# Last attention unit in four groups of four heads, and the mixing products over 128 rows

## What is computed

```python
h = einsum("bct,bcd->bdt", x, W[condition])           # a 32x32 mixing matrix per sequence
q = (h @ Wq_c.T + bq_c) @ Wq_up.T + bq_up             # 32 heads of 192
kv = h @ Wkv_c.T + bkv_c                              # 64 latent columns + 64 shared ones
scores = q . k / sqrt(192);  attn = softmax(scores)   # over the 32 tokens of a sequence
x = x + (attn @ v) @ Wo.T + bo                        # summed over the heads
x = x + ffn(convolution(x, taps), dequantised weights)
```

## Time and profile before

| | |
|---|---|
| median of 3 runs | 785.07 us |
| the profiled execution | 785.16 us |
| its span on the core | 783.4 us |
| PE busy (products) | 758.1 us, 97% |
| PE weight loads (PEld) | 599.0 us, 76% |
| DVE busy | 617.0 us, 79% |
| ACT busy | 377.4 us, 48% |
| GpSimd (POOL) busy | 199.1 us, 25% |

### The profile page before, as it was taken

The page is one execution under the profiler, slowest core; times in us unless marked ns, Lnnn a source line. Parts: engine busy times, 40 slices in busy tenths (PEclk is TensorE's granted clock), DMA queues, the critical chain, the costliest instruction groups (busy, mean ns, idle before and its releaser), DMA issues.

```text
span 783.4 us, 18621 instructions
## 1 busy us (share of the span) xinstructions
PE 758.1 (97%) x7821; PEld 599.0 (76%) x7821; DVE 617.0 (79%) x1109; ACT 377.4 (48%) x675; POOL 199.1 (25%) x203
## 2 busy tenths in 40 slices
PE   7999999999999999999999999999999699999996
PEld 5776777778677767868686777778676599999996
DVE  4476789988998786778777766968888578888887
ACT  2375546455563675565454636445674322222221
POOL 5002020011002000262200000000042388888871
PEclk9899999999999999999999999999999899999999
DMA  9910010010002000000400010002206159899861
GB/s 230 238 49 5 2 59 2 1 31 30 2 2 59 1 2 2 28 2 10 90 3 2 2 55 2 2 2 58 82 2 184 65 127 201 204 202 205 203 132 69
DMA packets 42739, 51.74 MB, mean 66 GB/s; under 512 B 7024, under 2 KB 29600, under 8 KB 42656
## 3 DMA queue, kind: packets, MB, share of 16 engines
q1 hardware_dynamic: 40384, 49.87, 25.9%
q0 software_dynamic: 1056, 0.49, 0.3%
q10 hardware_dynamic: 1216, 0.19, 0.1%
HBM read 41.91 MB, written 8.63 MB: 65 GB/s over the span
## 4 chain that ended last, share of the span: by engine, by line
PE 90%; DVE 5%; ACT 3%; issue 2%; another core or an unknown queue 1%; POOL 0%; DVEq 0%
PE ps L730 33%; PE ps L599 9%; PE ps L600 8%; PE ps L601 8%; PE ps L778 7%; PE ps L797 4%; PE ps L1063 4%; PE ps L1064 4%; PE ps L616 3%; PE ps L1032 2%; PE ps L693 1%; DVE z_low L1423 1%; PE ps L1020 1%; PE ps L1022 1%; PE ps L1021 1%
## 5 line engine op out<-in xcount | busy, mean ns | idle before, releaser
L1163 ACT ACTIVATE qt<-ps,m_bias 128x512 f32<-128x512 f32 x228 | 145.5, 684 | 96.4 <-PE ps L730 96.4
L730 PE MATMUL ps<-q_high,m_high 64*128 64x512 f32 x768 | 154.5, 398 | 2.4 <-ACT qt L1163 1.3
L730 PE MATMUL ps<-q_high,m_low 64*128 64x512 f32 x768 | 150.8, 388 | 0.0
L730 PE MATMUL ps<-q_low,m_high 64*128 64x512 f32 x768 | 108.3, 387 | 0.0
L1423 DVE TENSOR_TENSOR z_low<-ps,z_high 128x512 fp32r<-128x512 f32 x128 | 79.7, 682 | 15.9 <-ACT z_high L1182 15.9
L730 PEld LDWEIGHTS ps<-q_high,m_high 64*128 64x128 f32 x768 | 72.6, 184 | 24.5 <-issue 8.7
L730 PEld LDWEIGHTS ps<-q_low,m_high 64*128 64x128 f32 x768 | 72.7, 184 | 14.7
L529 POOL TENSOR_TENSOR o_sum<-o_part,o_part 128x512 f32<-128x512 f32 x7 | 9.1, 1303 | 294.0 <-ACT o_part L1192 294.0
L730 PEld LDWEIGHTS ps<-q_high,m_low 64*128 64x128 f32 x768 | 72.7, 185 | 13.6
L1182 ACT CAST z_high<-ps 128x512 fp32r<-128x512 f32 x128 | 66.8, 597 | 22.9 <-PE ps L797 22.9
L1168 ACT ACTIVATE sc<-sc 128x512 f32<-128x512 f32 x60 | 37.3, 631 | 46.6 <-DVE sc L1408 41.1
(11 more groups left out here) (292 smaller groups left out, 1646.0 us busy)
## 6 DMA issues: line engine op xcount, KB each, us to landing
x_in<-in_x SPq DMA_DIRECT2D x16, 512.0 KB, 3.6
x_s<-in_x SPq DMA_DIRECT2D x32, 256.0 KB, 5.7
out<-res SPq DMA_DIRECT2D x31, 256.0 KB, 3.6
toep_high<-taps_scratch SPq DMA_DIRECT2D x32, 192.0 KB, 4.3
toep_low<-taps_scratch SPq DMA_DIRECT2D x32, 192.0 KB, 5.0
toep_far<-taps_scratch SPq DMA_DIRECT2D x32, 64.0 KB, 5.5
wq_nope<-in_L_attn_Wq_up SPq DMA_DIRECT2D x2, 768.0 KB, 10.1
wq_nope<-in_L_attn_Wq_up SPq DMA_DIRECT2D x1, 1536.0 KB, 16.3
```

Of the source, the lines that this page charges most:

```text
L730: mm = pe.matmul(ps[:, fold_bank(u, j) + e, :], weights[rows, (GH * g + j) // 2, c, :], moving[c][rows, :], start=start, stop=stop)
L1163: act.activation(qt[:, j, :], ps[:, fold_bank(u, j) + j % 2, :], ACT.Identity, bias=m_bias[:, h:h + 1]).then_inc(s["qt_done"], 1)
```

## The change

It has two parts.

**Mixing.** `mixed_x(i)` makes 8 products of 128 rows and 128 columns. The two banks now hold two token quarters each, so the first bank is ready after half of the products; `mixed_high` and `mixed_low` copy 512 contiguous columns, and `project_ca` waits before its first and its third token quarter, for three and for four `h_low`.

**The last unit.** Its 16 heads go in four groups q of four. `scores_last(q)` makes 16 products of 128 columns into one bank, at least one pair of heads behind the fold of its group; `begun_last` and `ended_last` on DVE and `soft_last` on ACT treat one group; `values_last(h)` takes two groups and makes products of 64 columns. Units 14 and 15 use other PSUM banks, so some waits go or come.

```diff
+    LATE_ZBANK = ((BX, BZ, BZ + 1, BO), (BZ, BZ + 1, BT, BS))
-    LAST_SBANK = ((BS, BS + 1), (BZ, BZ + 1))
+    LAST_SBANK = (BX, BZ, BX, BT + 1)
...
-                for tt in range(TT):
-                    for g in range(2):
-                        for e in range(2):
-                            rows, o = slice(64 * e, 64 * e + 64), tt * P + 64 * g
-                            mm = pe.matmul(ps[:, MIX_BANK(i, e), o:o + 64], x_in[i % 2][rows, g, tt * P:(tt + 1) * P],
-                                           mix_of(i)[rows, g, rows], start=True, stop=True)
-                            if tt == TT - 1 and g == 1:
-                                mm.then_inc(s["h_ready"], 1)
+                for n in range(2):
+                    for t_ in range(2):
+                        for g in range(2):
+                            tt = 2 * n + t_
+                            o = t_ * HT + g * P
+                            mm = pe.matmul(ps[:, MIX_BANK(i, n), o:o + P], x_in[i % 2][:, g, tt * P:(tt + 1) * P],
+                                           mix_of(i)[:, g, :], start=True, stop=True)
+                    mm.then_inc(s["h_ready"], 1)
...
-                pe.wait_ge(s["h_low_done"], 4 * k + 4)
                 for tt in range(TT):
+                    if tt % 2 == 0:
+                        pe.wait_ge(s["h_low_done"], 4 * k + 3 + tt // 2)
                     mm = three(ps[:, BZ + 1, :], wcT_high[:, tt, 1, :], wcT_low[:, tt, 1, :], h_high[:, :, tt, :],
                                h_low[:, :, tt, :], tt == 0, tt == TT - 1)
...
-                    if u == LAST and j == GH // 2:
-                        pe.wait_ge(s["s_taken"], 4 * LAST + 4)
-                    if u == LAST and j == GH // 2 + 2:
-                        pe.wait_ge(s["zl_done"], 8 * (LAST - 1) + 6)
...
-            def scores_half(h, n):
-                pe.wait_ge(s["qt_done"], qt_count(LAST, 8 * h + 8))
-                if n == 0 and h == 1:
-                    pe.wait_ge(s["zl_done"], 8 * LAST)
-                for b in range(4):
-                    tok = slice((4 * n + b) * C, (4 * n + b + 1) * C)
-                    mm = pe.matmul(ps[32 * b:32 * b + 32, LAST_SBANK[h][n // 2], 256 * (n % 2):256 * (n % 2) + 256], kv[:, tok],
-                                   qt[:, 8 * h:8 * h + 8, tok], start=True, stop=True)
+            def scores_last(q):
+                pe.wait_ge(s["qt_done"], qt_count(LAST, 4 * q + 4))
+                if q == 0:
+                    pe.wait_ge(s["wfT_done"], 2 * TT)
+                    pe.wait_ge(s["s_taken"], 4 * LAST)
+                if q == 2:
+                    pe.wait_ge(s["zl_done"], 8 * (LAST - 1) + 1)
+                for n in range(4):
+                    for b in range(4):
+                        tok = slice((4 * n + b) * C, (4 * n + b + 1) * C)
+                        mm = pe.matmul(ps[32 * b:32 * b + 32, LAST_SBANK[q], P * n:P * n + P], kv[:, tok],
+                                       qt[:, 4 * q:4 * q + 4, tok], start=True, stop=True)
                 mm.then_inc(s["s_ready"], 1)
...
                     if u == LAST - 1:
-                        pe.wait_ge(s["wfT_done"], 2 * TT)
+                        pe.wait_ge(s["s_taken"], 4 * LAST + 2)
                 else:
                     if v == LAST:
-                        pe.wait_ge(s["qt_done"], qt_count(LAST, 6))
+                        pe.wait_ge(s["qt_done"], qt_count(LAST, GH - 1))
+                        pe.wait_ge(s["zl_done"], 8 * u + 3)
                     else:
                         pe.wait_ge(s["qt_done"], qt_count(v, GH - 2))
                         pe.wait_ge(s["qt_last"], 2 * v - 1)
-                    pe.wait_ge(s["zl_done"], 8 * u + 2)
+                        pe.wait_ge(s["zl_done"], 8 * u + 2)
...
             def values_last(h):
                 if h == 0:
                     pe.wait_ge(s["qt_done"], qt_count(NU, 0))
+                    pe.wait_ge(s["zl_done"], 8 * LAST)
+                    pe.wait_ge(s["s_taken"], 4 * NU)
                 else:
-                    pe.wait_ge(s["s_taken"], 4 * NU + 4)
                     pe.wait_ge(s["woT_done"], 1)
                     pe.wait_ge(s["zl_done"], 8 * LAST + 1)
-                value_block(LAST, h, lambda n: 4 * LAST + 4 * h + 2 * (n // 2) + 2,
-                            lambda rows, n, e: pT_last[h][rows, n, e:8:2, :])
+                for q in (2 * h, 2 * h + 1):
+                    pe.wait_ge(s["turn_done"], 4 * LAST + q + 1)
+                    for n in range(4):
+                        for b in range(4):
+                            rows = slice(32 * b, 32 * b + 32)
+                            for e in range(2):
+                                o = P * n + 64 * (q % 2)
+                                mm = pe.matmul(ps[64 * e:64 * e + 64, z_bank(LAST, h, b), o:o + 64], ctok[rows, n, :],
+                                               pT_last[q][rows, n, e:4:2, :], start=True, stop=True)
+                mm.then_inc(s["z_ready"], 1)
...
             def turned_wo():
                 pe.wait_ge(s["wo_in"], 16)
-                pe.wait_ge(s["zl_done"], 8 * LAST)
+                pe.wait_ge(s["s_taken"], 4 * LAST + 3)
                 for n in range(TT):
                     mm = pe.transpose(ps[:, BX, n * P:(n + 1) * P], wo_raw[:, n, :], ident[:])
                 mm.then_inc(s["woT_ready"], 1)
...
-            fold(LAST, 0, 8)
+            fold(LAST, 0, 6)
+            scores_last(0)
+            fold(LAST, 6, 10)
+            scores_last(1)
+            fold(LAST, 10, 12)
             values(LAST - 1, 0)
-            for n in range(4):
-                scores_half(0, n)
+            fold(LAST, 12, 14)
+            scores_last(2)
+            fold(LAST, 14, 16)
             values(LAST - 1, 1)
-            fold(LAST, 8, 12)
+            scores_last(3)
+            output(LAST - 1, 0)
+            output(LAST - 1, 1)
             turned_wo()
-            fold(LAST, 12, 16)
-            output(LAST - 1, 0)
-            for n in range(4):
-                scores_half(1, n)
-            output(LAST - 1, 1)
-            values_last(0)
             output(LAST - 1, 2)
             output(LAST - 1, 3)
+            values_last(0)
             output_last_high()
             values_last(1)
             for half in range(2):
...
             fold(LAST, 0, 4)
             part_taken(LAST - 2)
-            fold(LAST, 4, 8)
+            fold(LAST, 4, 10)
+            soft_last(0)
+            soft_last(1)
+            fold(LAST, 10, 12)
             values(LAST - 1, 0, 0, 4)
-            values(LAST - 1, 1, 0, 4)
-            fold(LAST, 8, 10)
-            soft_two(LAST, 0)
-            fold(LAST, 10, 12)
-            soft_two(LAST, 1)
+            fold(LAST, 12, 16)
+            values(LAST - 1, 1, 0, 2)
+            soft_last(2)
+            values(LAST - 1, 1, 2, 4)
             wo_high()
-            fold(LAST, 12, 16)
-            values(LAST, 0, 0, 1)
-            soft_two(NU, 0)
-            values(LAST, 0, 1, 3)
-            soft_two(NU, 1)
-            values(LAST, 0, 3, 4)
+            soft_last(3)
+            values(LAST, 0, 0, 4)
...
-            values(LAST - 1, 0, 0, 2)
-            take_two(LAST, 0)
-            take_two(LAST, 1)
-            values(LAST - 1, 0, 2, 4)
-            values(LAST - 1, 1, 0, 2)
-            below_two(LAST, 0)
-            values(LAST - 1, 1, 2, 4)
-            below_two(LAST, 1)
-            normalised_two(LAST, 0)
-            normalised_two(LAST, 1)
...
+            begun_last(0)
+            begun_last(1)
+            ended_last(0)
+            values(LAST - 1, 0, 0, 4)
+            ended_last(1)
+            begun_last(2)
+            values(LAST - 1, 1, 0, 4)
+            begun_last(3)
             dve.wait_ge(s["woT_high_done"], 1)
             dve.wait_ge(s["t_ready"], GH * NU)
             dve.tensor_tensor(woT_low[:], ps[:, BX, :], f(woT_high[:]), ALU.subtract).then_inc(s["woT_done"], 1)
-            for m_ in range(2):
-                take_two(NU, m_)
-            for m_ in range(2):
-                below_two(NU, m_)
+            ended_last(2)
             values(LAST, 0, 0, 4)
-            for m_ in range(2):
-                normalised_two(NU, m_)
+            ended_last(3)
             values(LAST, 1, 0, 4)
```

More of the change, by code:

```diff
@@ L1101, in mixed_high @@
             def mixed_high(i):
[L1102 to L1104 removed]
+                for n in range(2):
+                    act.wait_ge(s["h_ready"], 2 * i + n + 1)
+                    act.copy(h_high[:, i % 2, 2 * n:2 * n + 2, :].rearrange("p a n -> p (a n)"),
+                             ps[:, MIX_BANK(i, n), :]).then_inc(s["h_high_done"], 1)
             def projected_ca(k):
@@ L1374, in mixed_low @@
             def mixed_low(i):
-                for e in range(2):
-                    dve.wait_ge(s["h_high_done"], 2 * i + e + 1)
-                    dve.tensor_tensor(h_of(h_low, i, e), h_bank(i, e), f(h_of(h_high, i, e)),
+                for n in range(2):
```

(4 more changed lines are left out.)

65 lines of the change are left out of this document (27 added, 38 removed).

## The result

The changed kernel takes 776.22 us (median of four runs, 776.03 to 777.96), the kernel before 785.05 us beside it: a ratio of 0.9894, with a 95% interval of 0.9877 to 0.9911. The profiled execution has 776.39 us, 8.8 us less than that of before. The forecast was 782.3 us, and the range went down to 781.2 us.

The account below looks back on a forecast made before the run. PE work was taken to bound the kernel (90% of the last-ending chain). Start -1.6, last unit -1.2 and mixing 0 gave -2.8 us, against the median 785.07 a forecast of 782.3 us; range 781.2 to 785.8.

Parts of the forecast that it names:

- Mixing, costed at nothing: PE's mixing: 32 passes at 0.11 us in either form, so the seven later pairs were forecast to change by nothing.
- the rival of weight loads that do not hide: Mixing: whole-array weight loads are not hidden, 256 passes cost up to 28 us more, 810 us; chance 0.05.
- 0.15 us of start: Mixing before the change: part of a pair's 3.71 us, beside 32 pairs of passes at 0.111 us.
- The start, -1.6 us (ends -0.6 and -3.7): First projection: PE starts 0.6 us earlier and full clock returns at 23.15, 1.6 us saved; ends 0.6 and 3.7.
- the four `h_low` as a chain of 2.48 us: Start: four h_low, 0.61 us apart; waiting for three lets PE begin 0.6 us earlier, at about 18.95.
- My far end (0.65 + 3.05): Start: largest gain considered, 3.7 us, if there is no half-clock stretch at all.
- The last unit, -1.2 us: Last unit: output_last_low starts 0.7 us later, but its 24 products run at full clock and end 1.2 us earlier.
- told 0.3: Last unit: scores_last(2) waits for its z_low behind a normalisation and a rounding, costing 0.3 us.
- the 1.7 taken: Last unit: time for values_last(0), 1.7 us, taken between 1.2 if columns and 2.4 if pass issue set it.
- the clock falls in the new 3.2 us wait: Last unit, ahead of output_last_high: half speed costs 2.1 us, result -0.7 us, 784.4; chance 0.32 with or without start's gain.
- a stretch where PE was busy for 2.15 of 3.5 us at full clock: From 288.5 to 292.0 before the change: clock stayed at 1.00, used as evidence against a clock fall in the last unit.
- nothing moves: Start gain eaten by another late thing, last unit's by value blocks at 2.4 us: about -0.1, 785; chance 0.05.

Follow-up runs that it names:

- runs 5 to 8: One chip: changed kernel with values_last(0) earlier on PE, then also DVE, or unread products in one wait; kernel before with Wq loads held: 775.67, 775.19, 775.71, 781.46 us.
- run 2: Changed kernel with the old mixing, so the last unit's part of the change alone: 783.81 us, ratio to the kernel before 0.9994.
- run 7: Changed kernel with twelve unread 512-column products between values_last(0) and output_last_high, filling the 3.19 us wait: 775.71 us, ratio to the kernel before 0.9921.
- runs 5 to 7: Changed kernel with values_last(0) ahead of the last two outputs on PE; the same plus its z_low earlier on DVE; or twelve unread products instead: 775.67, 775.19, 775.71 us.
- run 9: Kernel before, unchanged, measured again on another chip: 784.74 us, ratio 0.9996.
- run 11: Kernel before with the loads of Wq held back until both first mixing calls are done: 785.01 us, ratio to the kernel before 0.9997.
- run 12: Changed kernel with values_last(0) ahead of the last two outputs on PE, its z_low earlier on DVE, five and eight unread products in two waits: 774.88 us.
- run 14: Changed kernel with six more one-column unread products in each of mixing calls 0 and 1: 780.87 us, ratio to the kernel before 0.9964.
- runs 9 and 15: Kernel before, unchanged: 784.74 us; kernel before with six instead of four warming products ahead of everything: 786.74 us.

## Why the prediction was wrong

**Mixing, costed at nothing: wrong, -2.3 us.** The 0.11 us a pass was right for both forms, and the rival of weight loads that do not hide did not come. The Trainium skill's rule that loads overlap only between row groups (TensorE: Matmul & The Clock Gate, "Part 3: Packing small matmuls — row/col tiling") does not hold for these products: 32 whole-array passes follow each other at 0.111 us. The step that failed is the "0.15 us of start". I took it for a cost of either form and began to count at the first pass. From there to the product behind, the pair took 3.49 us (95.74 to 99.23) and not 3.71, and another 0.10 us was saved ahead of the first pass, where I did not count. Both lie where PE changes to 64-row tiles and back: 0.33 us a pair.

**The start, -1.6 us (ends -0.6 and -3.7): direction right, -5.2 at `products(0)`, beyond the far end.** The step that failed took the four `h_low` as a chain of 2.48 us that only loses its last link. The rows ahead of it said that the chain itself began 2.5 us late: ACT's first `h_high` at 16.32, behind passes that ended at 13.8. With that gone, PE starts 2.4 us earlier, not 0.6, and behind the wait of 0.26 us the clock stays at 1.00: 2.8 us more, where I took 1.0. My far end (0.65 + 3.05) had the clock but not the earlier start. That the time was missed by so much is this step; why the increments come late, the runs do not show, and where they come in time (the chip of runs 5 to 8) the kernel before took 781.7 us and the three kernels with the new start 775.2 to 775.7, a smaller gain.

**The last unit, -1.2 us: -0.8 by the shift, and nothing by itself (run 2).** The pieces up to the outputs were 0.7 us better than told: `scores_last(2)` did not wait (told 0.3), the score blocks took 1.0 us each and `values(LAST - 1, 1)` waited 0.77, as told (1.0 and 0.8); the other 0.4 us I did not place. `values_last` took 1.59 us, near the 1.7 taken: 12.4 ns a pass of 64 columns against 19 ns of 128, so neither the columns alone nor the passes alone set the time. The waits of 3.2 and 2.0 us and `output_last_low` at 0.12 us a product came as told. The rival "the clock falls in the new 3.2 us wait" (chance 0.32) came true, at 1.4 us and not 2.1. Against it I had named a stretch where PE was busy for 2.15 of 3.5 us at full clock; the runs show how little that says: the wait of 2.00 us was passed at 1.00 in the changed kernel and at 0.50 in run 7.

**No rival reached the real time,** since none had the late `h_high` going away or the mixing getting faster. The rival "nothing moves" also has a slip: its terms, 0 for the start and -1.2 + 1.4 for the last unit, make +0.2 us and not -0.1.

## What to carry to other kernels

If a consumer's first row stands microseconds behind its producer's last one, price what a change does to that gap before what it does to the chain behind. Small products in row tiles that stand between whole-array products can cost time at both ends (here 0.33 us a pair of calls), so keep them together or widen them when the passes cost the same. In a stretch with several PE waits of one to three microseconds, removing one of them may only move the low clock to another, as in runs 5 to 7; here the gain came when all of them were gone or filled.

## What I had not expected of the hardware

PE's increments came 2.5 us behind the recorded end of the passes (kernel before: 13.8, ACT released at 16.32) and up to 2.9 (run 9), with the loads of Wq in flight or held back (run 11), in all traces of the start but the four on one chip. PE also stopped for 0.9 to 1.5 us with no wait to explain it: at the start before, in run 12 at 601.3, and in run 14 inside `values_last(0)`; in runs 9 and 15 it stopped at the start for 0.2 to 0.5 us at a time. The clock was 0.50 in the last unit of every trace with a wait or gap above 1 us there (3.4, 6.8 or 10.2 us in all), and 1.00 throughout in the two without.
